# A transformer block on one core: the prologue's loads on one queue, the first layer norm shared by two engines, and batch 1's norm and the gate placed earlier

## What is computed

```python
mod = (_silu(L0_c) @ L0_wmod).reshape(4, 6, 1, -1)
sa, ca, ga, sb, cb, gb = (mod[:, i] for i in range(6))
ga = (2 * (ga >= 0) - 1) * jnp.maximum(jnp.abs(ga), 0.25)   # gb alike
h = _layernorm(x) * (1 + ca) + sa
x = x + ga * attention(h, W_K, W_Q, W_V, W_O)    # 16 heads of 128, causal
h = _layernorm(x) * (1 + cb) + sb
x = x + gb * ffn(h, ...)    # top-2 of 8 experts, a shared expert, a core branch
```

## Time and profile before

| | us |
|---|---|
| median of 3 runs | 843.75 (842.40 to 844.26) |
| the profiled execution's own time | 843.71 |
| its span, first to last instruction | 841.9 |
| outside the span | 1.8 |
| PE busy in the span | 800.9 (95%) |
| DVE busy | 680.8 (81%) |
| ACT busy | 628.3 (75%) |
| POOL busy | 450.2 (53%) |

### The profile page before, as it was taken

The page is one execution under the profiler, slowest core; times in us unless marked ns, Lnnn a source line. Parts: engine busy times, 40 slices in busy tenths (PEclk is TensorE's granted clock), DMA queues, the critical chain, the costliest instruction groups (busy, mean ns, idle before and its releaser), DMA issues.

```text
span 841.9 us, 14484 instructions
## 1 busy us (share of the span) xinstructions
PE 800.9 (95%) x4822; PEld 713.0 (85%) x4822; DVE 680.8 (81%) x1639; ACT 628.3 (75%) x1404; POOL 450.2 (53%) x311
## 2 busy tenths in 40 slices
PE   7778999999999999999999999999999599999997
PEld 6657978999999999999999999998998587788786
DVE  4686998888888888888888788889898787877776
ACT  4566778878887788788887887787877488686874
POOL 3064455664444655544466544575465555566753
PEclk7979999999999999999999999999999799999999
DMA  7233223334222433332234332344222220212131
GB/s 243 72 89 107 63 63 88 88 97 111 63 64 65 112 94 88 91 89 66 64 89 108 100 88 63 78 107 129 65 63 64 69 84 18 76 51 80 47 114 38
DMA packets 47449, 70.54 MB, mean 84 GB/s; under 512 B 5520, under 2 KB 38448, under 8 KB 47248
## 3 DMA queue, kind: packets, MB, share of 16 engines
q1 hardware_dynamic: 46720, 68.28, 30.8%
q0 software_dynamic: 368, 0.81, 0.3%
q10 hardware_dynamic: 288, 0.53, 0.2%
HBM read 25.49 MB, written 2.17 MB: 33 GB/s over the span
## 4 chain that ended last, share of the span: by engine, by line
PE 75%; ACT 9%; DVE 8%; issue 3%; POOL 2%; DMA 2%; SPq 0%; DVEq 0%; POOLq 0%; ACTq 0%
PE M L681 16%; PE M L680 16%; PE M L682 16%; PE S L680 7%; PE S L682 6%; PE S L681 6%; ACT PB L591 3%; PE T L680 2%; PE T L682 2%; PE T L681 2%; ACT PB L626 1%; DVE tmp L1025 1%; DVE S L1060 1%; DVE gab L1076 1%; ACT pth L650 1%
## 5 line engine op out<-in xcount | busy, mean ns | idle before, releaser
L547 POOL TENSOR_TENSOR ptl<-ptl,pth 128x640 fp32r<-128x640 f32 x128 | 198.9, 1576 | 45.0 <-ACT pth L650 45.0
L591 ACT ACTIVATE PB<-S,nb 128x128 f32<-128x128 f32 (+3 forms) x256 | 133.8, 532 | 114.0 <-DVE nb L1060 114.0
L540 POOL TENSOR_TENSOR X<-X,fb 128x512 f32<-128x512 f32 x64 | 83.2, 1301 | 252.1 <-DVE fb L1089 252.1
L626 ACT ACTIVATE PB<-PB,ri 128x256 f32<-128x256 f32 (+3 forms) x256 | 124.4, 579 | 9.4 <-DVE ri L1069 9.3
L1049 DVE TENSOR_TENSOR qk<-M,qk 128x512 fp32r<-128x512 f32 x128 | 88.1, 689 | 53.5 <-ACT qk L639 53.5
L1060 DVE CUSTOM_DVE_ANT_0 S<-S,cc 128x128 f32<-128x128 f32 (+3 forms) x256 | 117.5, 521 | 2.3 <-PE S L682 2.3
L1076 DVE STREAM_TRANSPOSE gab<-PB 128x256 f32<-128x256 f32 (+2 forms) x192 | 109.5, 623 | 1.1 <-ACT PB L626 0.6
L680 PE MATMUL M<-hh,W 128*128 128x512 f32 x264 | 103.8, 393 | 0.2 <-DVE hl L1035 0.2
L681 PE MATMUL M<-hl,W 128*128 128x512 f32 x264 | 103.3, 391 | 0.0
L682 PE MATMUL M<-hh,W 128*128 128x512 f32 x264 | 103.1, 391 | 0.0
L680 PE MATMUL S<-qk 128*128 128x128 f32 (+3 forms) x256 | 88.0, 344 | 4.6 <-DVE qk L1049 4.6
(11 more groups left out here) (181 smaller groups left out, 2310.5 us busy)
## 6 DMA issues: line engine op xcount, KB each, us to landing
ptl<-gab SPq DMA_DIRECT2D x256, 160.0 KB, 3.1
stage<-in_wat SPq DMA_DIRECT2D x16, 512.0 KB, 4.9
gab<-scw SPq DMA_DIRECT2D x16, 256.0 KB, 3.3
tmp<-scw SPq DMA_DIRECT2D x16, 256.0 KB, 3.5
X<-in_x SPq DMA_DIRECT2D x4, 512.0 KB, 5.3
stage<-in_wfa SPq DMA_DIRECT2D x3, 512.0 KB, 4.4
out<-X SPq DMA_DIRECT2D x3, 512.0 KB, 2.6
X<-in_wmod SPq DMA_DIRECT2D x1, 1024.0 KB, 6.5
```

Source lines behind the costliest of these rows:

```text
L540: pool.tensor_tensor(X[:, a:a + 512], X[:, a:a + 512], fb[:, c2 * 512:c2 * 512 + 512], ALU.add).then_inc(s_y, 1)
L547: pool.tensor_tensor(ptl[u % 2][:, s], ptl[u % 2][:, s].bitcast(F32), pth[u % 2][:, s].bitcast(F32), ALU.subtract).then_inc(s_pl, 1)
L591: ins = act.activation(PB[:, P_OFF[i]:P_OFF[i] + w], PS[bk][:, a:a + w], ACT.Exp, bias=nb[:, i:i + 1], scale=-1.0, accum_out=sm[:, i:i + 1])
L626: act.activation(p, p, ACT.Copy, scale=ri[:, i:i + 1]).then_inc(s_P3, 1)
```

## The change

- **Loads.** SP issues x of batch 0 in two halves, the identity, the first part of `wmod` (which ACT's queue loaded before), weight pieces 0 and 1, the constants, x of batch 1 and the rest of `wmod`, one behind the other. Batch 1 and the rest of `wmod` stood behind the load of piece 3 before.
- **Norm of batch 0.** A new event `nb` computes minus mean times inverse deviation on DVE; with it ACT writes half of `nm` of batch 0 with Identity (scale and bias), and all of batch 1's (`ACT_NM`). `nm` of batch 0 and `mod` stand ahead of `wh` 0 and `wh` 1.
- **Piece 1.** POOL casts the high half (instead of ACT), DVE subtracts for the low half (instead of POOL).
- **Order.** Batch 1's `st` and `nm` stand in the list's head, `mg` ahead of S of unit 1, `v` of pair 0 behind S of unit 0, batch 1's `h` in iteration 0 and `ms` behind z of unit 0. POOL's low half of piece 3 stands ahead of the low half of unit 1's probabilities. The gate takes four POOL instructions instead of five, and its last transfer is an event of its own, `mh`.
- **Experts' biases.** `b1` moves behind the first `dn` (the down projection of the expert stage), `d0` into the expert stage, chunks 2 to 4.
- **Fillers.** `WARM` is 60, 16, 12.

```diff
@@ attention_plan
-    put(post, 0, ("mg",))
-    put(post, 1, ("ms",))
+    put(post, 0, ("ms",))
...
-            fill[i] = [[("st", b, 0), ("st", b, 1)], [("st", b, 2)], [("st", b, 3)], [("nm", b, 0), ("nm", b, 1)]]
-            put(post, i, ("h", b, 0), ("h", b, 1))
+            put(pre, i, ("h", b, 0))
+            put(post, i, ("h", b, 1))
...
-    fill[20] = [[("d0", 0)], [("d0", 1)], [], [], [("d0", 2)]]
...
+        ("q", 0), ("st", 1, 0), ("st", 1, 1), ("k", 0), ("wh", 2), ("ld", 4), ("S", 0), ("st", 1, 2), ("st", 1, 3),
...
+            plan += [("dn", 0), ("b1",)]
@@ ffn_plan
+    for k in range(3):
+        put(0, 2 + k, ("d0", k))
@@
-BY_V = (0, 21, 22)
+BY_V = (0, 1, 21, 22)
+ACT_NM = ((0, 1), (1, 0), (1, 1))
@@ SP
-            load_x(0)
+            for n, done in enumerate((s_x[0], s_xh)):
+                sp.dma_start(X[:, 512 * n:512 * n + 512], x[:, 512 * n:512 * n + 512]).then_inc(done, 16)
+            sp.dma_start(cc[:, 0:128], cst[:, 0:128]).then_inc(s_id, 16)
+            sp.dma_start(PB[:, 0:1024], wmod[:, 0:1024]).then_inc(s_wm, 16)
             load(0)
-            sp.dma_start(cc[:, 0:128], cst[:, 0:128]).then_inc(s_id, 16)
             load(1)
             sp.dma_start(cc[:, 128:], cst[:, 128:]).then_inc(s_c, 16)
+            load_x(1)
+            sp.dma_start(X[:, 2048:4096], wmod[:, 1024:3072]).then_inc(s_wm2, 16)
...
-                elif ev[0] == "wh":
-                    n = ev[1]
-                    if n == 2:
-                        sp.dma_start(X[:, 2048:4096], wmod[:, 1024:3072]).then_inc(s_wm2, 16)
-                        load_x(1)
@@ POOL, the gate
-                    pool.tensor_scalar(g2, rg, 0.0, 2.0, ALU.is_ge, ALU.mult).then_inc(s_gr, 1)
+                    pool.tensor_scalar(g2, rg, 0.0, 0.5, ALU.is_ge, ALU.subtract).then_inc(s_gr, 1)
                     pool.wait_ge(s_gr, 1)
-                    pool.tensor_scalar(g2, g2, -1.0, None, ALU.add).then_inc(s_gr, 1)
+                    pool.tensor_tensor(g1, rg, g2, ALU.mult).then_inc(s_gr, 1)
                     pool.wait_ge(s_gr, 2)
-                    pool.tensor_tensor(g1, rg, g2, ALU.mult).then_inc(s_gr, 1)
+                    pool.tensor_scalar(g1, g1, 0.125, 4.0, ALU.max, ALU.mult).then_inc(s_gr, 1)
...
+                if ev[0] == "mh":
                     pool.wait_ge(s_gd, 32)
@@ POOL, piece 1
+                if ev == ("wh", 1):
+                    _, slot, a, w = piece(1)
+                    pool.wait_ge(s_st[1], 16)
+                    pool.tensor_copy(wt(slot, a, w)[0], stage[:, 1024:2048]).then_inc(s_w1, 1)
@@ ACT
-            act.dma_start(PB[:, 0:1024], wmod[:, 0:1024]).then_inc(s_wm, 16)
...
+                elif kind == "nm" and ev[1:] in ACT_NM:
...
+                    act.wait_ge(s_nb, n + 1)
+                    if n and k == 0:
+                        act.wait_ge(mf, tmp_read[n - 1])
+                    for c in (2 * k, 2 * k + 1):
+                        s = slice(b * 1024 + 256 * c, b * 1024 + 256 * c + 256)
+                        ins = act.activation(tmp[:, 256 * c:256 * c + 256], X[:, s], ACT.Identity,
+                                             bias=rs[:, 8 + c:9 + c], scale=rs[:, 4 + c:5 + c])
+                    ins.then_inc(s_xn, 1)
@@ DVE
+                elif kind == "nb":
...
+                    v.scalar_tensor_tensor(out=rs[:, 8:12], in0=mv[:, 0:8:2], scalar=-1.0, in1=rs[:, 4:8],
+                                           op0=ALU.mult, op1=ALU.mult).then_inc(s_nb, 1)
```

58 lines of the change are left out of this document (33 added, 25 removed), and 5 rows, old and new, of the table plan.

## The result

The changed kernel takes **830.95 us** (median of four executions, 828.41 to 832.40) against 844.0 (842.4 to 845.93) before: ratio 0.9841, 95% interval 0.9805 to 0.9877. In a later comparison with more executions it was 832.01 (828.02 to 832.82) against 844.0, ratio 0.9837, 0.9811 to 0.9864. It is faster, as forecast, and lies 3.9 us above the 827.1 forecast, inside the range. Its profiled execution took 829.57.

The account below looks back on a forecast made before the run. PE was taken as busy nearly everywhere, losing time up to 84 us to pauses and low clock, with DVE as the spine. From 843.71: -16.8 - 0.5 + 0.7 = -16.6, so 827.1 us; 80% range 823.6 to 831.6.

Parts of the forecast that it names:

- the wait for batch 2's x: DVE's 4.65 us stall until 78.92 goes; batch 2's statistics start at 62.15, 16.8 us earlier.
- the walk: Step-by-step timing of the new program up to batch 2's statistics, using the old trace's distances between handoffs; 16.8 us earlier.
- I take `wmod` at 6.3; at the worst at 8.2 as before: At the start, `wmod` lands at 6.3 us on SP's single queue, at the worst at 8.2.
- a queue that moves 414 GB/s needs no help: Leaving ACT's queue costs no rate; if a second queue added bandwidth, the sum would lose up to 1.9 us.
- so PE goes on without a pause, and `mod` runs at the full clock: After the first fillers, `mod` takes 1.90 us instead of 3.55 at half clock and ends at 8.8.
- The first transfers are late: Rival: x and `wmod` land as before, pieces 0 and 1 late; `mod` starts 1.3 us later, 828.5 to 830; 10%.
- the pauses still take the clock: Rival: short PE pauses cause two or three clock falls, 1.6 us each; +3.2 to +4.8, 830.3 to 831.9; 17%.
- The signs that the prediction named: Wrong if the clock falls in 11 to 18 or behind 33, POOL's cast exceeds 3.8, or unit-4-to-attention-end time grows.
- a full clock from 12 us on: Sign expected in the new profile: PE's granted clock at 1.00 from 12 us on.
- My term of 0.5 for the clock in 80 to 84: PE's low clock in 80 to 84 us goes; gain between 0 and 1.5 us, taken as 0.5.
- `d0`: 0.7 taken: Moving `d0` into the expert stage, where DVE is on the path, loses 0 to 2.0 us, taken as 0.7.
- the premise that `d0` "cost nothing": In its old place, a stretch bound by PE, `d0` cost no time.

Follow-up runs that it names:

- identity late: Changed kernel with the identity's load issued behind `wmod` and weight piece 0 instead of ahead of `wmod`; 831.13 us, one execution.
- Gelu first: Changed kernel with the Gelu over the experts' biases (`b1`) back at the head of the list; 833.44 us, one execution.
- norm on DVE: Changed kernel with batch 1's norm on DVE instead of ACT, batch 0's still shared; 830.28 us, one execution.
- V ahead: Changed kernel with the first V product back ahead of the first scores; 835.84 us, one execution.
- 92 fillers: Changed kernel with 92 instead of 60 fillers (multiplications of zeros on PE) at the start; 829.37 us, one execution.
- ACT's queue: Changed kernel with the first part of `wmod` issued on ACT's queue again, all else on SP's; 830.32 us, one execution.
- fillers in every wait: Changed kernel with fillers in every PE pause its trace shows up to 52 us; 830.35 us, five executions, ratio to before 0.9830.
- more fillers: Fillers in every wait, with 38 instead of 18 ahead of `ms`, plus the late fillers; 828.93 us, five executions, ratio 0.9824.
- small loads late: The more-fillers kernel with POOL's four small table loads issued only once `wmod` has landed; 827.40 us, five executions, ratio 0.9810.
- the late fillers: Kernel before, with 96 and 30 fillers in PE's two late waits for expert weights; 843.29 us against 843.57, ratio 0.9994.

## Why the prediction came out as it did

**The direction and the bulk: right.** The three long pauses, the stretched norm (0.73 us for DVE's two instructions beside an idle POOL) and the wait for batch 2's x went as the walk had it. Distances hold within 0.3 us up to unit 2: modulation to unit 0's mask 8.95 forecast, 9.15 measured; to unit 1's 10.45 and 10.37; to unit 2's 8.45 and 8.17. POOL's cast took 1.88 (bounds 1.2 and 3.9, taken 2.4). Batch 2's load was issued at 52.4 instead of 48.3 and still nobody waited for it.

**The step that failed: "I take `wmod` at 6.3; at the worst at 8.2 as before".** It landed at 8.20. I had argued that a queue that moves 414 GB/s needs no help, but the rate in the first microseconds is not that: 156 to 402 GB/s, by halves of a microsecond, from 2.5 to 8 us. Then the next sentence, "so PE goes on without a pause, and `mod` runs at the full clock", fell with it: 1.65 of pause, `mod` 1.2 longer, sixteen fillers 0.8 longer, transposes at half clock. The late landing by itself is priced by the second profile of the changed kernel, where the clock held through `mod`: landing at 8.35, modulation at 12.04, so about 1.6 for the landing, and 1.9 more for the clock.

**The two rivals that held together.** "The first transfers are late" had the landing but priced it at 1.3; "the pauses still take the clock" had the price but put it behind the pauses at the scores of units 0 and 2 and between 11 and 18 us. The first two came (1.42 and 2.00), and the clock did fall behind the second; the costly fall came earlier, at 8.8, behind the pause for `wmod`. By the prediction's own prices, a late landing (1.4 to 2.9) and one fall (1.6) on top of 827.1 give 830.1 to 831.6, and the median of 830.95 lies there. I had kept the two apart, as if one excluded the other. A late transfer makes a pause, and so they come together. The Trainium skill, TensorE: Matmul & The Clock Gate, "A second HAM failure mode: psum-queue depth-cycling", tells of a kernel whose short pauses between groups made the clock swing; the traces here agree so far as falls came behind pauses of 1.65, 2.00 and 1.1 to 1.2, though not in every execution.

**The signs that the prediction named.** One of them came: it called itself wrong if the clock fell in 11 to 18 or behind 33 us, and the clock was at 0.50 from 8.8 to 15.6 and from 39.5 to 42.9. So the time is inside the range although the claim of a full clock from 12 us on failed; part of that is luck, since the fall at 39.5 cost nothing and the first profile has none between 48 and 60. The other signs held: POOL's cast took 1.88, not over 3.8, the longest pause of PE was 2.00, and from unit 4's mask to that of unit 63 it took 570.98 us instead of 576.22.

**What a fall costs depends on where it is.** From the mask of unit 2 to that of unit 4, the profiles of the changed kernel and its variants, which have the same work there but for fillers:

| at 0.50 within 48 to 60 us | unit 2 to unit 4, us | which |
|---|---|---|
| none | 21.34 | changed kernel, first profile |
| 3.4 us | 22.26 to 22.42 | identity late, Gelu first, norm on DVE, V ahead |
| 6.8 us | 23.85 to 23.88 | 92 fillers, ACT's queue, changed kernel second profile |
| 3.4 us, 32 fillers added | 23.35 | fillers in every wait |
| none, 52 fillers added | 22.14, 22.41 | more fillers, small loads late |

So 1.0 us for the short fall and 2.5 for the long one: PE leads here. Only one profile has no fall and no fillers, so the base of 21.34 rests on one execution. In the three with added fillers, 0.8 to 1.1 us are lost again ahead of `ms`, where DVE waits 0.5 to 1.0 for ACT or a transfer; so they came out ahead only of the long fall. The fall at 39.5 in the changed kernel costs nothing: 12.66 us from unit 2's mask to unit 3's is what the run with V ahead took too, at the full clock up to 56. The one at 654 to 665 before (the late fillers) costs at most the 1.9 that the interval allows. My term of 0.5 for the clock in 80 to 84 was as uncertain; the measured gain behind the statistics is 0.

**`d0`: 0.7 taken, 0.25 at most measured.** Its three instructions took 0.45, 0.23 and 0.31 us. The shift of 14.35 at the first Gelu of the expert stage, ahead of them, is 14.13 at the first weighted product behind. The last of them is the one that had taken 1.47. But the premise that `d0` "cost nothing" where it stood was wrong too: the gain is 14.19 us at the masks of units 20 to 22, 15.59 at unit 23's, behind the place where `d0`'s last instruction had stood (262.5), 14.99 at unit 24's and 14.61 from unit 36's on. So about 0.4 was won by taking it out of the attention; another 0.3 is lost between unit 63's mask and the expert stage's first Gelu, and the cause of that isn't shown.

**The spread between executions.** The ten executions of the changed kernel lie at 828.0 to 829.6 (four) and 831.8 to 832.8 (six), with mean clocks of 0.988 to 0.990 and 0.982 to 0.986. The profiles show one fall that goes with it: a stretch of 3.4 us at half clock near 704 us, in seven of the fourteen profiles. From batch 2's statistics to the end these seven take 765.68 to 766.58 us, the seven without it 763.73 to 764.88, a mean difference of 1.85. The changed kernel's first profile is without, its second with. The two differ by 1.6 behind the statistics and by 0.6 at them (65.38 against 64.74), together the 2.2 us between them. The three kernels with the late fillers have no such stretch in their profiles, and the two on the changed kernel have the narrow spreads of 2.1 and 2.2 us; but so has the kernel with fillers in the prologue only, 2.2, with the stretch in its profile. In the kernel before the late fillers changed the median by 0.3 us only; its interval allows 1.9. There 7 of 17 executions lie above 845 us without them and none of 12 with them. So the 1.85 goes with the stretch; that the stretch causes it is not shown.

**Left open.** Why `wmod` lands 5.4 to 6.7 us after its issue from one profile to the next: neither the identity's pieces nor POOL's loads do it, and a queue of its own only shifts the wait to x. And why the same program's clock holds behind a pause of 2.26 us in one execution and falls behind 1.65 in another. In these two the fillers' change from 107 to 56 ns comes at 4.46 and at 5.42; whether that has to do with it isn't shown.

## What to carry over

A transfer taken at its best while its worst is known to be 2 us away is a rival with a pause behind it, and a pause brings the clock along: price the two as one case. Before paying for fillers, find out who leads in the stretch where the clock falls; the same 3.4 us at half clock cost 1.0 us where PE led and nothing that shows where DVE led. And look first for an instruction on an in-order engine that waits for its operand with ready work behind it: moving one such event was worth about 4 of 14 us, by one execution.
